# Layer norm high parts on three engines, the bias added before a store, and the order of the filter products

## What is computed

```python
def _layernorm(x, eps=1e-5):
    return (x - mean(x)) / sqrt(var(x) + eps)

h = maximum(_layernorm(x), 0.0);  x = x + gat_gru(h, adj, ...)      # layer 0
h = maximum(_layernorm(x), 0.0);  x = x + gcn(h, adj, W)            # layer 1
h = maximum(_layernorm(x), 0.0)                                     # layer 2
Z = ...                                # two steps of attention and diffusion
x = x + (_layernorm(h + Z) * ln_g + ln_b)
h = maximum(_layernorm(x), 0.0)                                     # layer 3
node = h @ W1                                                       # N x 32
hw = einsum('nc,kcf->nkf', h, W2)                                   # N x 32 x 256
y = einsum('nk,nkf->nf', node, hw)
x = x + relu(adj @ y + node @ b)
```

## Time and profile before

| | us |
|---|---|
| Median of 3 runs | 2990.27 (2988.0 to 2992.92) |
| The profiled execution, its own time | 2988.41 |
| The profiled execution, span | 2986.7 |
| Norm with parts, rows started to last low part, each of four | about 21.4 |
| Norm ln2b, block start to last statistics | 2268.7 to 2317.4 |
| keys0 | 771.9 to 838.3 |
| Filters, first matmul to last low part | 2346.4 to 2871.3 |

### The profile page before, as it was taken

How to read it: one execution, slowest core, us unless ns; L and a number is a source line. 1 busy time by engine, 2 the same in 40 slices (tenths; PEclk the granted TensorE clock), 3 DMA queues, 4 the chain that set the end, 5 groups by cost and what they waited for, 6 DMA issues and landing times. The chain is left out here.

```text
span 2986.7 us, 44231 instructions
## 1 busy us (share of the span) xinstructions
PE 2314.8 (78%) x14310; PEld 1703.0 (57%) x14310; DVE 1941.0 (65%) x4668; ACT 1224.8 (41%) x1981; POOL 662.2 (22%) x1649
## 2 busy tenths in 40 slices
PE   3499999589536999996844974877563599999999
PEld 2377777377315787775523763766462244444468
DVE  5567777523337877777238888888965577777741
ACT  3455566211346666661256863766422100000000
POOL 2000000200224444340025643555402200000000
PEclk9699999899768999998966987989787799999999
DMA  1322221054100000000100000000004000000013
GB/s 46 119 98 97 97 81 68 5 191 145 42 17 13 19 23 19 22 27 14 48 17 6 16 11 11 16 11 16 11 11 155 2 1 0 0 0 0 0 50 96
DMA packets 49299, 120.85 MB, mean 40 GB/s; under 512 B 5952, under 2 KB 24672, under 8 KB 45792
## 3 DMA queue, kind: packets, MB, share of 16 engines
q1 hardware_dynamic: 49120, 118.83, 11.8%
HBM read 93.85 MB, written 24.97 MB: 40 GB/s over the span
## 5 line engine op out<-in xcount | busy, mean ns | idle before, releaser
L1923 DVE SCALAR_TENSOR_TENSOR fil_acc<-bank,fil_node,fil_acc 128x256 f32<-128x256 f32 x682 | 330.0, 484 | 110.4 <-PE bank L1991 97.8
L1346 PE MATMUL bank<-idf,X 128*128 128x128 f32 x968 | 136.2, 302 | 202.9 <-DVE step_recips L1841 202.9
L1436 ACT ACTIVATE step_PT<-bank 128x512 f32<-128x512 f32 (+1 forms) x264 | 127.5, 577 | 357.4 <-PE bank L1346 357.4
L1989 PE MATMUL bank<-parts_in,fil_xTh 128*128 128x512 f16 x704 | 268.5, 381 | 0.0
L1991 PE MATMUL bank<-parts_in,fil_xTl 128*128 128x512 f16 x704 | 268.3, 381 | 0.0
L1990 PE MATMUL bank<-parts_in,fil_xTh 128*128 128x512 f16 x704 | 268.2, 381 | 0.0
L1346 PEld LDWEIGHTS bank<-idf,X 128*128 128x128 f32 x968 | 119.4, 154 | 215.4 <-DVE step_recips L1841 206.2
L722 PE MATMUL bank<-V,HL 128*128 128x256 f32 x968 | 236.4, 386 | 0.2
L1356 PE MATMUL bank<-kH,qHL 128*128 128x512 f16 (+1 forms) x264 | 105.9, 401 | 151.9 <-ACT step_E L1445 117.7
L1378 PE MATMUL bank<-A,step_PT 128*128 128x256 f32 x968 | 216.1, 379 | 0.0
L1378 PE MATMUL bank<-H,step_PT 128*128 128x256 f32 x968 | 216.0, 379 | 0.0
(11 more groups left out here) (382 smaller groups left out, 5044.4 us busy)
## 6 DMA issues: line engine op xcount, KB each, us to landing
gat_A<-in_adj SPq DMA_DIRECT2D x22, 1408.0 KB, 5.9
step_a<-adjT SPq DMA_DIRECT2D x44, 352.0 KB, 3.0
gcn_raw<-in_L_W SPq DMA_DIRECT2D x16, 512.0 KB, 4.7
split<-gcn_halves SPq DMA_DIRECT2D x16, 512.0 KB, 3.4
parts_in<-split SPq DMA_DIRECT2D x4, 2048.0 KB, 19.2
adjT<-gat_a SPq DMA_DIRECT2D x22, 352.0 KB, 2.3
gcn_a<-adjT SPq DMA_DIRECT2D x22, 352.0 KB, 3.9
out_a<-adjT SPq DMA_DIRECT2D x22, 352.0 KB, 2.9
```

The costliest lines, as they stand in the source:

```text
L1346: last = pe.transpose(p_bank[n % nb][:, i * 128:i * 128 + 128], M[j][:, (b + i) * 128:(b + i) * 128 + 128], core.idf[:])
L1436: act.activation(PT[:, b * 128:(b + m) * 128], p_bank[n % len(p_bank)][:, 0:m * 128], ACT.Copy).then_inc(pT_done, 1)
L1923: c(dve.scalar_tensor_tensor(out=acc[k][:], in0=ps, scalar=node[k][:, n:n + 1], in1=acc[k][:], op0=ALU.mult, op1=ALU.add))
L1989: pe.matmul(w_bank[n % 4][:], xTh[k][:, x], wh[:, blk], start=c == 0, stop=False)
```

## The change

Layer norm: the high part of tile t is made by GpSimd (t mod 3 = 0), ScalarE (1) or VectorE (2), each with its own semaphore, and the loops of ScalarE and VectorE are written out. ln2b loads only the gain, and the kept input in four loads of 5, 6, 5 and 6 tiles with a semaphore each; GpSimd does nothing in it. keys0 loads the bias, GpSimd adds it to `X`, and the store of `X` waits for that. Filters: TensorE does the first eight banks of `products` right after `transposes`, then `nodes` and `bias`, then the other eight; VectorE's `bias` comes after `weigh`. In this order the low parts of a norm follow the high parts one tile behind.

```diff
@@ -38,6 +38,7 @@
 NL = len(LCH)
 SH = 1024.0
 LOADS = 4
+FIRSTS = [T * n // LOADS for n in range(LOADS)]
 SG = 64.0
 SX = 8.0
 SW = 4096.0
@@ -222,24 +223,27 @@
     with nc.cleanup_on_exit(), ExitStack() as ctx:
         sem = {k: nc.alloc_semaphore(f"{name}_{k}")
                for k in ("stats_done", "aggregated", "var_ready", "root_ready", "newton", "scales_ready",
-                         "rows_done", "by_ready", "hi_done", "affine_loaded", "shifted", "affine_steps", "added",
+                         "rows_done", "by_ready", "affine_loaded", "affine_steps", "added",
                          "x_counted")}
         sb = lambda n, s, d=F32: core.sb(f"{name}_{n}", s, d, ctx)
+        hi_done = [nc.alloc_semaphore(f"{name}_hi_done{n}") for n in range(3)]
         stats = core.stats
         mv = sb("mv", [128, T * 2])
         ve, rstd, nmr, root, ta, tb = (sb(n, [128, T]) for n in ("ve", "rstd", "nmr", "root", "ta", "tb"))
         by = sb("by", [128, T])
-        if affine:
-            gb = [sb(n, [128, D]) for n in ("g", "b")]
+        if affine is not None:
+            gain = sb("g", [128, D])
+            kept_loaded = [nc.alloc_semaphore(f"{name}_kept_loaded{n}") for n in range(LOADS)]
         block = ctx.enter_context(nc.Block())
 
-        if affine:
+        if affine is not None:
             @block.sync
             def _(sp):
-                for a, dram in zip(gb, affine):
-                    sp.dma_start(a[:], dram.partition_broadcast(128)).then_inc(sem["affine_loaded"], 16)
-                sp.dma_start(X[:].rearrange("p (t f) -> p t f", t=T),
-                             x_kept.rearrange("(t p) f -> p t f", p=128)).then_inc(sem["affine_loaded"], 16)
+                sp.dma_start(gain[:], affine.partition_broadcast(128)).then_inc(sem["affine_loaded"], 16)
+                for n in range(LOADS):
+                    part = slice(T * n // LOADS, T * (n + 1) // LOADS)
+                    sp.dma_start(X[:].rearrange("p (t f) -> p t f", t=T)[:, part, :],
+                                 x_kept.rearrange("(t p) f -> p t f", p=128)[:, part, :]).then_inc(kept_loaded[n], 16)
                 if weights:
                     parts_in, split, weights_loaded = weights
                     for n in range(4):
@@ -270,15 +274,21 @@
             dve.scalar_tensor_tensor(out=nmr[:], in0=m[:, 0, :], scalar=-1.0, in1=rstd[:],
                                      op0=ALU.mult, op1=ALU.mult).then_inc(sem["scales_ready"], 1)
 
+            def high(t, k):
+                if t % 3 == 2:
+                    dve.wait_ge(sem["rows_done"], t + 1)
+                    dve.tensor_scalar(hi(HL, t), cols(H, t), cols(by, t, 1), None, ALU.mult).then_inc(hi_done[2], 1)
+
             def low(t, k):
-                dve.wait_ge(sem["hi_done"], t + 1)
+                dve.wait_ge(hi_done[t % 3], t // 3 + 1)
                 dve.scalar_tensor_tensor(out=lo(HL, t), in0=cols(H, t), scalar=cols(by, t, 1), in1=hi(HL, t),
                                          op0=ALU.mult, op1=ALU.subtract)
 
             def scale_and_add(t, k):
+                if t in FIRSTS:
+                    dve.wait_ge(kept_loaded[FIRSTS.index(t)], 16)
                 dve.wait_ge(sem["rows_done"], t + 1)
-                dve.wait_ge(sem["shifted"], t + 1)
-                dve.tensor_tensor(cols(H, t), cols(H, t), gb[0][:], ALU.mult).then_inc(sem["affine_steps"], 1)
+                dve.tensor_tensor(cols(H, t), cols(H, t), gain[:], ALU.mult).then_inc(sem["affine_steps"], 1)
                 dve.wait_ge(sem["affine_steps"], t + 1)
                 dve.tensor_tensor(cols(X, t), cols(X, t), cols(H, t), ALU.add).then_inc(sem["added"], 1)
 
@@ -286,23 +296,13 @@
                 dve.wait_ge(sem["added"], t + 1)
                 dve.bn_stats(cols(stats, t, 6), cols(X, t)).then_inc(sem["x_counted"], 1)
 
-            if affine:
-                dve.wait_ge(sem["affine_loaded"], 48)
+            if affine is not None:
+                dve.wait_ge(sem["affine_loaded"], 16)
                 dve.wait_ge(sem["aggregated"], T)
-                pipelined(dve, [(0, scale_and_add), (1, count)])
+                unrolled(dve, [(0, scale_and_add), (1, count)])
                 dve.wait_ge(sem["x_counted"], T)
             if parts:
-                pipelined(dve, [(0, low)])
-
-        if affine:
-            @block.gpsimd
-            def _(pool):
-                pool.wait_ge(sem["affine_loaded"], 48)
-
-                def shift(t, k):
-                    pool.tensor_tensor(cols(X, t), cols(X, t), gb[1][:], ALU.add).then_inc(sem["shifted"], 1)
-
-                pipelined(pool, [(0, shift)])
+                unrolled(dve, [(0, high), (1, low)])
 
         if parts:
             @block.gpsimd
@@ -310,8 +310,9 @@
                 pool.wait_ge(sem["by_ready"], 1)
 
                 def high(t, k):
-                    pool.wait_ge(sem["rows_done"], t + 1)
-                    pool.tensor_scalar(hi(HL, t), cols(H, t), cols(by, t, 1), None, ALU.mult).then_inc(sem["hi_done"], 1)
+                    if t % 3 == 0:
+                        pool.wait_ge(sem["rows_done"], t + 1)
+                        pool.tensor_scalar(hi(HL, t), cols(H, t), cols(by, t, 1), None, ALU.mult).then_inc(hi_done[0], 1)
 
                 unrolled(pool, [(0, high)])
 
@@ -325,7 +326,14 @@
                 act.activation(cols(H, t), cols(src, t), ACT.Relu if relu else ACT.Identity,
                                bias=cols(nmr, t, 1), scale=cols(rstd, t, 1)).then_inc(sem["rows_done"], 1)
 
-            pipelined(act, [(0, rows)])
+            def high(t, k):
+                if t % 3 == 1:
+                    act.wait_ge(sem["rows_done"], t + 1)
+                    act.activation(hi(HL, t), cols(H, t), ACT.Copy, scale=cols(by, t, 1)).then_inc(hi_done[1], 1)
+
+            if parts:
+                act.wait_ge(sem["by_ready"], 1)
+            unrolled(act, [(0, rows), (1, high)] if parts else [(0, rows)])
 
 
 def load_weight(sp, sem, dst, dram, rows=128):
@@ -886,7 +894,7 @@
             unrolled(dve, [(0, scale), (2, add), (3, statistics), (2, low)])
 
 
-def keys(core, name, src, kH, kL, qHL, shape, W1, W2, W3, x_kept=None, pending=None):
+def keys(core, name, src, kH, kL, qHL, shape, W1, W2, W3, x_kept=None, pending=None, shift=None):
 
 
     nc = core.nc
@@ -915,6 +923,8 @@
         row = [sb(f"row{k}", [128, CB * ROW]) for k in range(2)]
         qT = sb("qT", [DA, NP])
         valid = sb("valid", [128, 1])
+        if x_kept is not None:
+            added, added_loaded, shifted = sb("added", [128, D]), sem("added_loaded"), sem("shifted")
         gram = sb("gram", [DA, MOMENT])
         scr = sb("scr", [128, T * DA])
         mean, square, root = (sb(n, [128, T]) for n in ("mean", "square", "root"))
@@ -931,6 +941,8 @@
                 sp.dma_start(wk[:].rearrange("p (c n) -> p c n", n=128)[:, :, h * DA:h * DA + DA],
                              W3.rearrange("(c p) n -> p c n", p=128)).then_inc(loaded, 16)
             if x_kept is not None:
+                sp.dma_start(added[:], shift.partition_broadcast(128)).then_inc(added_loaded, 16)
+                sp.wait_ge(shifted, T)
                 sp.dma_start(x_kept.rearrange("(t p) f -> p t f", p=128),
                              core.X[:].rearrange("p (t f) -> p t f", t=T)).then_inc(saved, 16)
                 sp.wait_ge(saved, 16)
@@ -947,6 +959,13 @@
             pool.affine_select(out=valid[:], in_=valid[:], compare_op=ALU.is_ge, fill=0.0,
                                base=N - 1 - (T - 1) * 128, pattern=[[0, 1]],
                                channel_multiplier=-1).then_inc(ones_done, 1)
+            if x_kept is not None:
+                pool.wait_ge(added_loaded, 16)
+
+                def shift_rows(t, k):
+                    pool.tensor_tensor(cols(core.X, t), cols(core.X, t), added[:], ALU.add).then_inc(shifted, 1)
+
+                pipelined(pool, [(0, shift_rows)])
 
         @block.tensor
         def _(pe):
@@ -1932,7 +1951,7 @@
                 dve.wait_ge(nb_ready, t + 1)
                 dve.tensor_scalar(cols(H, t), n_bank[k][:, D:], 1.0, None, ALU.mult).then_inc(nb_done, 1)
 
-            pipelined(dve, [(2, bias), (2, weigh), (3, low), (0, lows)])
+            pipelined(dve, [(2, weigh), (2, bias), (3, low), (0, lows)])
 
         @block.scalar
         def _(act):
@@ -1977,11 +1996,12 @@
                 pe.wait_ge(node_done, t * 2 + 2)
                 pe.matmul(n_bank[k][:, D:], nodeT[k][:], bsb[:], start=True, stop=True).then_inc(nb_ready, 1)
 
-            def products(t, k):
-                pe.wait_ge(xT_lo, t + 1)
-                if isinstance(t, int) and t == 0:
-                    pe.wait_ge(weights_loaded, 64)
-                for n in range(W3C):
+            def products(t, k, part):
+                if part == 0:
+                    pe.wait_ge(xT_lo, t + 1)
+                    if isinstance(t, int) and t == 0:
+                        pe.wait_ge(weights_loaded, 64)
```

(8 more changed lines are left out.)

## The result

The changed kernel takes **2928.37 us** (median of 4 runs, 2927.83 to 2930.16) against 2990.22 us (4 runs, 2988.0 to 2992.92): ratio 0.9784, interval 0.9772 to 0.9797, 61.9 us saved. The profiled execution took 2928.72 us (span 2926.9), 59.8 us of span less than before. The forecast was 51.1 us and 2939 us, with a range from 2930: the direction came as said and each part gained, or cost nothing, where it was said to, but more time went than the sum had. Most of what it lacked lies in the filters, which lost 21.65 us where the forecast had 13.4.

A forecast was written before the change was run, and what follows sets the result against it. No engine is full, so each stage has its own limit. Norms 22.4, ln2b 15.3, filters 13.4, keys 0 sum to 51.1 us off 2988.41, giving 2937.3; the runs' median lies 1.86 higher, so 2939 us, range 2930 to 2957.

The forecast's parts named there:

- 15.8 us forecast: Each of the four norms with high parts in turn takes 15.8 us against 21.4, 5.6 saved.
- Rival 1: In the norms GpSimd and VectorE exclude each other: about 19 us a norm, 2.4 saved, 2952 us; chance 0.2.
- 17.1 instead of 15.3: ln2b without bias work or GpSimd wait, input in four loads: 15.3 us saved, bounds 13 and 17.5.
- 22 x 1.25: VectorE's pace in ln2b: 22 tiles at 1.25 us, 27.5 us in all.
- Rival 3: In ln2b the first quarter lands with the whole load, at 2283.5: 9 us lost, 2948 us; chance 0.06.
- right at nothing: Bias added in the keys stage costs 0, bounds 0 and 2 us; the store lands with 30 us of cover.
- part 4's 13.4 us: Filters: first eight products follow the transposes, node and bias matmuls in the middle; 13.4 us saved, bounds 8 and 15.4.
- the hole closed by products: Filters, tile border: TensorE's node products wait for ScalarE's copies, an avoidable 0.77 us a tile that products would fill.
- 20 x (0.77 - 0.10): Filters: 20 borders, each gaining the 0.77 us wait less 0.10 for the new seam, 13.4 us.
- The 0.10 for the new seam: Filters, mid-tile: the moved node and bias matmuls cost 0.1 us a tile, at best nothing, at worst 0.35.
- Rival 4: TensorE's granted clock falls in the denser filters, 20.7 us more a tile; five tiles give 3043 us; chance 0.02.
- Rival 2: Filters' gain given back by seam gaps or mid-tile stalls: half stays, 2946 us, or none, 2952; chance 0.12.

The follow-up runs named there:

- the run with two engines: Changed kernel with the norms' high parts made by GpSimd (even tiles) and VectorE (odd tiles), none by ScalarE: 2927.48 us, ratio 0.9783.
- the run with the loop: Changed kernel with VectorE in ln2b awaiting all four loads and its three operations a tile in a hardware loop: 2939.35 us.
- The run with the old first tile: Changed kernel, but in the filters' first tile all 16 banks come after the node and bias matmuls, as before: 2929.98 us.
- ln2b alone: Kernel before with only ln2b without the bias and in four loads, and the bias added in keys0: 2975.41 us, ratio 0.9948.
- the norms written out: Kernel before with only the loops of ScalarE and VectorE in the four norms written out; GpSimd still makes all high parts: 2990.79 us.
- parts alone: Kernel before with only the high parts in turn on three engines in the four norms: 2969.37 us, ratio 0.9917.

## Why the prediction was right or wrong

1. **The norms: right.** 15.8 us forecast, 15.73, 15.69, 15.69 and 15.55 measured; four norms give 22.8 against 22.4, and the part alone 22.0. ScalarE at 0.49 a copy and 0.40 a step was the value taken: 19.25 - 18.85 = 0.40. The Trainium skill (ScalarE: Activation LUTs, "What ACT_TABLE_LOAD costs") says that each operand taken by pointer adds about 93 ns to an ACTIVATE and that ACTIVATEs back to back overlap by about 93 ns; the trace agrees: the row operation has two such operands and takes 0.585 us, this copy has one and takes 0.49, at 0.40 a step. What I had wrong inside it is who pays for GpSimd and VectorE together. I let VectorE's low parts grow to 0.69 as in the earlier trace rows and kept GpSimd at 0.92. Here the lows stayed near 0.5 and GpSimd went to 1.41. ScalarE, which waits for neither of them, sets the pace at 1.89 us for three tiles. That the sum met the measurement within 0.1 us is partly luck: the seven periods took 13.2 us instead of 13.7, and the end behind them, with its GpSimd operation of 1.41, 2.5 instead of 2.1. Rival 1 (19 us a norm, 2952 us) is refuted by the norm's length, and more plainly by the run with two engines, 14.7 us where exclusion needs 22.1.

2. **ln2b: the mechanism right, two sizes off, 17.1 instead of 15.3.** The start was 6.8 us after the block's first issue, I had 5.7: the first quarter took 6.2 us from an issue 0.4 after that, and the three loads behind it took up to 10.1. The term that was mis-sized is the pace, 22 x 1.25. I read 1.25 us a tile from the loop and named 1.15 "written out rather than looped" only as a bound, though the diff shows the loop written out. It was 1.12, 2.9 us in all, and the run with the loop gave 2.8 back. Rival 3 (the first quarter lands with the whole) is refuted: that state is the run that waits for all four, and it costs 6.7 us, not 9, since even the whole input landed 13.3 us after the block and not 14.8 as before.

3. **Keys: right at nothing.** The adds took 0.68 us each, not 0.85, the cover was 35 us and not 30, the stage 66.51 against 66.40. The 69.7 us of some kernels has nothing to do with this part: of the two in the table one has only the high parts changed, the other only the filters, and the kernel with this part alone has 66.49.

4. **Filters: the step of the prediction that failed, part 4's 13.4 us; measured 21.65.** The mechanism, the hole closed by products, was right. The sum 20 x (0.77 - 0.10) had one term of the wrong sign and left out two others. Without these 8.3 us the total would have stayed inside the range.
The gain per border was put at 0.77 - 0.10 = 0.67 and was 0.85. The hole was read at one border with 0.66 us of idle time; 17 of the 20 have 0.60, so it is nearer 0.72 in the mean. The 0.10 for the new seam, taken for a price that the trace doesn't have, had the wrong sign: in the middle of a tile the first node matmul's weights load behind a product, and the group costs 1.64 instead of 1.75. The bounds below it, from nothing to 0.35, left out that a moved group could get cheaper. 20 x 0.18 = 3.6 us.
The first tile was counted at nothing. Its node matmuls ran at the granted clock of 0.50 in the trace, and I had looked only at the steady stretch. The run with the old first tile puts 2.3 us on its order (one execution; 1.4 to 2.9 by the spread of the stage).
The fall of the clock before tile 20 was counted at nothing too and gave 1.7 us. I wrote that the clock stayed at 1.00 before; that is so for the 200 us of the earlier trace rows, not for the end. Of five traces with the old order four show the fall, 0.50 over 3.4 us (the kernel before, its repetition, ln2b alone and the norms written out), and take 46.76 us from tile 19 to tile 21; parts alone keeps 1.00 and takes 45.08; of the seven with the new order none falls, and they take 44.8 to 44.9. Rival 4, the clock falling in denser filters, had the sign reversed: here the low level came after a hole, and the denser stage kept 1.00. Since the forecast had no such term, its absence is an oversight; that the same hole can also pass without a fall makes this part of the gain chance.
What is left of the 8.3 us above the forecast is 0.7, of which 0.4 lies behind the first weighing of tile 21. Rival 2 is refuted: no gap at any seam, no wait of TensorE from 2330 to 2811.

5. **The rest.** Norms +0.4, ln2b +1.8, filters +8.3 make 10.5 us more than the 51.1, so 61.6, and the span lost 59.8. The 1.8 us between are the stages in which nothing was meant: step0 4.5 shorter, step1 3.3 longer (the profiled execution of before had a short one, 749.04 against 752.64 in its repetition), gat and gcn giving back 2.5 of what their norms saved. The medians of the kernel before in the sets of runs go from 2990.2 to 2994.2 us, so a microsecond or two of a sum is not to be explained by rows of one execution. The range ended at 2930 because its low end had 15.4 for the filters (58.9 us in all, which makes 2931.4); each of the three terms of point 4 was outside that bound.

## What to carry to other kernels

When a group of instructions is moved on a pipelined engine, price it again at its new place, with its weight load and the granted clock there, and let the bound go below its old price. Read the start and the end of a stage as closely as its steady middle: here 4 us of 21.65 came from the first tile and from one fall of the clock near the end, and both stood in the trace of before. What the start costs differs from execution to execution: the first weighing of tile 1 came 31.3 to 32.8 us into the stage in the six traces with the new order. Give an engine that slows beside another (GpSimd at 1.4 instead of 0.9 us) less work or none as soon as the pace is set elsewhere, and keep it off the last tile.

## What was not expected of the hardware

- GpSimd and VectorE on the same buffers: before, GpSimd held 0.92 us and VectorE's operations grew (0.69, 0.82); after, VectorE nearly held (0.37 and 0.51 in the mean, 0.35 and 0.48 with GpSimd idle) and GpSimd grew to 1.41; with two engines sharing the high parts, both grew a little (1.14, 0.46). The sum of their work overlaps by far in each case.
- Three operations a tile in a hardware loop on VectorE cost 0.13 us more than written out, from 1.12 to 1.25.
- The granted clock came to the full level 5.0 to 8.0 us after the first matmul of the filters with the products early (6.6 in the changed kernel, 2307.75 to 2314.3), and 10.3 to 12.2 us after it with node matmuls first (10.8 before, 2346.35 to 2357.1).
- The same 0.92 us of idle time, followed by the same matmuls, was followed by 3.4 us at the 1.2 GHz level in four traces and by none in a fifth. A fall cost 1.7 us.
- keys0 takes either 66.4 to 67.0 or 69.7 us, and step0 607 to 610 or 613 to 616 us, in kernels whose work in these stages is alike (but for the bias adds in keys0). For step0, writing out loops of other blocks was enough in the one execution of that kernel. Why stays open.
